# Layer 1 of a four-layer graph kernel: GpSimd's low half of x waits for the last residual of a group

## The chip, the cores and the metric

The kernel runs on one core of a Trainium2 chip, in one launch. The metric is device microseconds from the start to the end of that launch. Five engines have instruction streams of their own and meet only at semaphores: TensorE (PE in the profile), VectorE (DVE), ScalarE (ACT), GpSimd (POOL) and SyncE (SP), which here issues DMAs.

## The reference, cut to what matters

x has 64 graphs of 128 nodes with 256 features, adj has 64 matrices of 128x128. Four layers follow each other, each with a residual and a layer norm. The change lies in the second of them, which the kernel calls layer 1:

```
qk = einsum('bnd,ed->bne', x, W_qk); q, k = split(qk, 2)
v = einsum('bnd,ed->bne', x, W_v)
scores = einsum('bnd,bmd->bnm', q, k) / 8
w = softmax(sum(scores * adj, axis=-1, keepdims=True), axis=1)
x = layernorm(x + w * v)
```

The others are a hypergraph convolution (layer 0), a three-hop diffusion (layer 2) and an attention with tanh scores (layer 3).

## The kernel before

x stays in SBUF as one resident f32 tile `K.x` (`x_resident` in the profile). The work goes in groups of `GP` = 4 graphs, so there are `G` = 16 groups g = 0 to 15, and most tiles exist twice and are used in turn (p = g % 2).

f32 products are made of f16 pairs. A layer needs, for each group, a high and a low half of x, both transposed. ScalarE makes the high half (`x_high`, L1118: a copy that rounds to f16), GpSimd makes the low one (`x_low`, L1125: x minus the high half, a TENSOR_TENSOR over 128x1024 whose two inputs both lie in SBUF). SyncE then transposes each half with one DMA (`transpose_x`, L1139) into `xT_hi` and `xT_lo`, and `project` on TensorE waits for both. One product is then three matmuls (`triple`, L110 to L112). The halves are made ahead: layer 1 makes those of groups 2 to 15, and with numbers 16 and 17 those of the first two groups of layer 2.

Every engine runs a hand-written list of steps (`over_layers`): the first four unrolled, the middle ones in a hardware loop, the last ones unrolled and woven with the first steps of the next layer. The order inside a step is fixed, and an engine does not pass a wait. What belongs together in layer 1, when VectorE is in its step g:

- VectorE, step g: `weights(g-1)` copies four columns of softmax weights out of PSUM (L1282); `residual(g-1, j)` for j = 0 to 3 (L1288) computes vqk * weight + x into `l_pre`, a SCALAR_TENSOR_TENSOR of 128x256 with two inputs in SBUF; two rows of norm statistics (`norm_row`, L1039, one SBUF input); `scores(g)` (L1296, L1297 from PSUM and vqk, then L1302 reduces to `l_w`); two more rows of statistics; `maximum(g)` (L1306, L1310), `norm_variance(g-1)` (L1046 to L1053) and `softmax(g)` (L1314, L1318).
- TensorE at the same time, its step g+1: `aggregate(g)` (L1213, eight records), `project(g+1, 0)` and `project(g+1, 1)` (12 matmuls), `score_rows(g)` (L1221, waits for `l_w`), `project(g+1, 2)` and `project(g+1, 3)` (12 matmuls), `weight_columns(g)` (L1225), which releases VectorE's next L1282.
- ScalarE, step g: `x_high(g+2)`, four times `norm_apply(g-2)` (L1073), `exponentials(g)` (L1256), four times `copy_qkv(g+1)` (L1250).
- GpSimd, step g: `x_low(g+2)`, then `norm_scales(g-1)` (L1058 to L1067).
- SyncE, step g: the two transposes of group g+2, then the DMA that brings the adjacency of group g+2 (L1181).

Each `residual` adds one to the semaphore `L.pre_ok` (`l1_pre_ok`), so it stands at `upto(g, GP, 4)` = 4g + 4 when the four residuals of group g are done. `reused(g, 3)` is true in the loop and for g of 3 or more.

Of the kernel before, what the change touches and what calls it, by code (L numbers as in the profile page):

```python
# [12 lines left out]
GP = 4  # L13
# [24 lines left out]
def upto(g, per, k):  # L38

    return g * per + k  # L40
# [62 lines left out]
def reused(g, back=2):  # L103

    return not isinstance(g, int) or g >= back
# [901 lines left out]
def norm(nc, ctx, tag, deep=2, tiles=None):  # L1007

    L = Parts()
    L.deep = deep  # L1010
    tiles = tiles or ctx

    def sb(name, shape):
        made = [tiles.enter_context(nc.sbuf_tensor(f"{tag}_{name}{i}", shape, F32)) for i in range(deep)]
        return [made[p % deep] for p in range(2)]

    L.pre, L.st = sb("pre", [128, GP, D]), sb("st", [128, GP, 6])
    L.veps, L.rstd, L.nmr = (sb(name, [128, GP]) for name in ("veps", "rstd", "nmr"))
    L.mdiff, L.m2, L.dd, L.msum, L.mneg = (tiles.enter_context(nc.sbuf_tensor(f"{tag}_{name}", [128, GP], F32))
                                           for name in ("mdiff", "m2", "dd", "msum", "mneg"))  # L1020
    L.pre_ok, L.st_ok, L.agg, L.mean_ok, L.rstd_ok, L.nmr_ok, L.x_new = (
        ctx.enter_context(nc.semaphore(f"{tag}_{name}"))
        for name in ("pre_ok", "st_ok", "agg", "mean_ok", "rstd_ok", "nmr_ok", "x_new"))
    return L
# [31 lines left out]
def norm_scales(K, L, pool, g, p):  # L1056
    pool.wait_ge(L.st_ok, upto(g, GP, GP))
    pool.tensor_tensor(L.msum[:], L.st[p][:, :, 1], L.st[p][:, :, 4], ALU.add).then_inc(L.mean_ok, 1)  # L1058
    pool.wait_ge(L.mean_ok, upto(g, 2, 1))
    pool.tensor_tensor(L.mneg[:], L.msum[:], K.minus_half[:], ALU.mult).then_inc(L.mean_ok, 1)  # L1060
    pool.wait_ge(L.agg, upto(g, 4, 4))
    if reused(g, L.deep):
        pool.wait_ge(L.x_new, upto(g - L.deep, GP, GP))
    pool.tensor_tensor(L.rstd[p][:], L.veps[p][:], K.minus_half[:], ALU.pow).then_inc(L.rstd_ok, 1)  # L1064
    pool.wait_ge(L.mean_ok, upto(g, 2, 2))
    pool.wait_ge(L.rstd_ok, upto(g, 1, 1))
    pool.tensor_tensor(L.nmr[p][:], L.mneg[:], L.rstd[p][:], ALU.mult).then_inc(L.nmr_ok, 1)  # L1067
# [26 lines left out]
def front_of(shared, layer):  # L1094
    F = Parts()
    F.x_hi, F.x_lo, F.xT_in, F.xs, F.xT = shared.x_hi, shared.x_lo, shared.xT_in, shared.xs, shared.xT
    F.base = (layer - 1) * G
    F.made = 2
    F.ahead = 2 if layer < 3 else 0
    return F  # L1100


def halves_due(F, g):

    return not isinstance(g, int) or F.made <= g < G + F.ahead


def x_group(K, g):

    return K.x[:, xcols(g - G if isinstance(g, int) and g >= G else g)].rearrange("p (g d) -> p g d", g=GP)  # L1110
# [10 lines left out]
def x_low(K, F, pool, g, p):  # L1121
    pool.wait_ge(F.x_hi, upto(F.base + g, 1, 1))
    if reused(F.base + g):
        transposed(F, pool, g - 2, p)
    pool.tensor_tensor(F.xs[p][1], x_group(K, g), F.xs[p][0], ALU.subtract).then_inc(F.x_lo, 1)  # L1125


def transposed(F, eng, g, p):

    eng.wait_ge(F.xT_in[p], 16 * (F.base + g - p) + 32)  # L1130
# [12 lines left out]
def layer1(nc, K, ctx, tiles):  # L1143
# [10 lines left out]
    L = norm(nc, ctx, "l1", tiles=tiles)  # L1154
# [16 lines left out]
    F = front_of(K.F, 1)  # L1171
# [172 lines left out]
        return step, 0, 1  # L1344

    def gpsimd(pool):
        def step(g, p, has):
            q = 1 - p
            if halves_due(F, g + 2):
                x_low(K, F, pool, g + 2, p)  # L1350
            if has(-1):
                norm_scales(K, L, pool, g - 1, q)
        return step, 2, 1
# [611 lines left out]
```

## Time and profile before

| | us |
|---|---|
| three runs | 774.9, 776.5, 778.07 |
| median | 776.5 |
| the profiled execution, as timed | 778.61 |
| its span in the trace | 776.8 |
| PE busy in the span | 696.9 (90%) |
| DVE busy | 588.0 (76%) |
| ACT busy | 531.9 (68%) |
| POOL busy | 343.3 (44%) |
| mean granted TensorE clock | 0.948 |

Layer 1 fills about 303 to 446 us of the span. The first L1282 starts at 314.9 us and the sixteenth and last at 444.4 us, one for each group. TensorE's granted clock has two levels in this trace, 1.00 (2.4 GHz) and 0.50 (1.2 GHz); a number between them is a mean over a stretch.

### The profile page before, as it was taken

The page shows a single profiled execution, that of the slowest core. Times are in us where ns is not written, and L with a number is a line of the kernel's source. Part 1 is how long each engine was busy: PE and PEld are TensorE (multiplying, and loading weights), DVE is VectorE, ACT ScalarE, POOL GpSimd, SP SyncE. Part 2 cuts the span into 40 slices and gives each one's busy share as a digit, 9 for nine tenths or more (in the row PEclk, how much of TensorE's full clock was granted, in tenths as well). Part 3 has the DMA queues.
Part 4 walks back from the last instruction along what each step waited for, and adds up shares of the span by engine and source line. Part 5 has one row for each costly group of instructions (what it writes and reads, how often), then busy time and mean ns, then how long its engine had stood idle before and what let it go on. Part 6 is the DMA issues. An engine that isn't in the chain of part 4 may idle for free.

```text
span 776.8 us, 18723 instructions
## 1 busy us (share of the span) xinstructions
PE 696.9 (90%) x5654; PEld 504.1 (65%) x5654; DVE 588.0 (76%) x1744; ACT 531.9 (68%) x1177; POOL 343.3 (44%) x418
## 2 busy tenths in 40 slices
PE   5899999999999985777878589899989998999995
PEld 5677777777777753444445366566666666888874
DVE  4888888888878762777887876767676876588995
ACT  4668887767777763465555557667776776688885
POOL 2243455434344451444444425243524253677773
PEclk9999999999999997997797689999999999799998
DMA  9522032232221020643444334634343333266663
GB/s 285 154 84 70 29 109 69 73 117 83 68 68 54 2 53 30 149 83 81 95 89 100 55 55 82 83 77 87 81 82 81 81 73 65 55 164 162 162 145 128
DMA packets 168144, 71.11 MB, mean 92 GB/s; under 512 B 122260, under 2 KB 165654, under 8 KB 168088
## 3 DMA queue, kind: packets, MB, share of 16 engines
q1 hardware_dynamic: 166496, 70.41, 37.8%
q8 instruction: 28, 0.46, 0.3%
q10 hardware_dynamic: 1592, 0.01, 0.1%
q14 instruction: 28, 0.23, 0.1%
HBM read 28.46 MB, written 8.39 MB: 47 GB/s over the span
## 4 chain that ended last, share of the span: by engine, by line
PE 39%; DVE 8%; issue 6%; DMA 4%; ACT 2%; SPq 1%; DVEq 1%; POOL 0%; ACTq 0%; POOLq 0%
PE bank L110 10%; PE bank L112 10%; PE bank L111 10%; DMA xT_lo<-x_halves 4%; PE bank L1804 3%; DVE l_pre L1288 2%; DVE l_st L1039 2%; PE bank L1407 2%; PE bank L1802 1%; SPq L1139 1%; PE bank L1225 1%; PE bank L1513 1%; DVE l_w L1302 1%; DVE l_qa L1296 1%; ACT x_resident L1073 1%
## 5 line engine op out<-in xcount | busy, mean ns | idle before, releaser
L1073 ACT ACTIVATE x_resident<-l_pre,l_nmr,l_rstd 128x256 f32 (+1 forms) x256 | 136.9, 595 | 26.8 <-POOL l_nmr L1067 26.7
L1125 POOL TENSOR_TENSOR x_halves<-x_resident,x_halves 128x1024 f16<-128x1024 f16 (+1 forms) x46 | 100.1, 2176 | 39.2 <-ACT x_halves L1118 37.1
L110 PE MATMUL bank<-Wk_lo,xT_hi 128*128 128x2 f16 (+2 forms) x384 | 94.0, 274 | 4.8 <-DMA xT_lo<-x_halves 4.8
L1039 DVE BATCH_NORM_STATS2 l_st<-l_pre 128x6 f32<-128x256 f32 x256 | 96.5, 413 | 1.1
L111 PE MATMUL bank<-Wk_hi,xT_lo 128*128 128x2 f16 (+2 forms) x384 | 95.1, 273 | 0.0
L112 PE MATMUL bank<-Wk_hi,xT_hi 128*128 128x2 f16 (+2 forms) x384 | 94.7, 272 | 0.0
L983 POOL TENSOR_TENSOR hq<-hq 128x512 f32<-128x512 f32 x32 | 43.1, 1347 | 76.6 <-ACT hq L716 76.6
L1064 POOL TENSOR_TENSOR l_rstd<-l_veps,minus_half 128x4 f32<-128x4 f32 x64 | 64.6, 1009 | 24.1 <-DVE l_veps L1053 22.7
L110 PE MATMUL bank<-W2T_lo,h_hi 128*128 128x257 f16 x256 | 70.7, 276 | 2.3 <-DVE h_lo L860 1.2
L111 PE MATMUL bank<-W2T_hi,h_lo 128*128 128x257 f16 x256 | 70.8, 277 | 0.0
L112 PE MATMUL bank<-W2T_hi,h_hi 128*128 128x257 f16 x256 | 70.8, 276 | 0.0
L1729 POOL TENSOR_TENSOR l_T_lo<-l_tf,l_T_hi 128x512 f16<-128x512 f32 x16 | 18.5, 1157 | 106.6 <-ACT l_T_hi L1573 106.6
L860 DVE TENSOR_TENSOR h_lo<-hf,h_hi 128x512 f16<-128x512 f32 x64 | 44.7, 702 | 18.9 <-ACT hf L705 8.3
L1288 DVE SCALAR_TENSOR_TENSOR l_pre<-l_vqk,l_wgt,x_resident 128x256 f32<-128x256 f32 x64 | 55.0, 922 | 1.9 <-DVE l_wgt L1282 1.7
L722 ACT ACTIVATE zf<-bank 128x258 f32<-128x258 f32 x64 | 24.7, 388 | 46.2 <-PE bank L637 46.1
L705 ACT ACTIVATE hf<-bank,b_col 128x512 f32<-128x512 f32 x64 | 44.0, 687 | 16.1 <-PE bank L112 15.6
L110 PE MATMUL bank<-qkvT_lo,xT_hi 128*128 128x384 f16 x128 | 48.0, 375 | 6.2 <-PEq L527 6.2
L110 PE MATMUL bank<-xT_lo,W1T_hi 128*128 128x512 f16 x128 | 48.5, 379 | 1.6 <-DVE qkvT_lo L414 1.5
L112 PE MATMUL bank<-xT_hi,W1T_hi 128*128 128x512 f16 x128 | 48.5, 379 | 0.0
L111 PE MATMUL bank<-xT_hi,W1T_lo 128*128 128x512 f16 x128 | 48.5, 379 | 0.0
L1118 ACT ACTIVATE x_halves<-x_resident 128x1024 f16 (+1 forms) x46 | 48.4, 1052 | 0.0
L971 POOL TENSOR_TENSOR zrs<-zvar,minus_half 128x4 f32<-128x4 f32 x16 | 22.0, 1378 | 59.0 <-DVE zvar L897 59.0
(206 smaller groups left out, 2119.6 us busy)
## 6 DMA issues: line engine op xcount, KB each, us to landing
adj<-in_adj SPq DMA_DIRECT2D x32, 256.0 KB, 3.7
x_halves<-in_x SPq DMA_DIRECT2D x16, 512.0 KB, 3.7
x_resident<-in_x SPq DMA_DIRECT2D x16, 512.0 KB, 4.8
out<-x_resident SPq DMA_DIRECT2D x15, 512.0 KB, 3.2
l_adjT<-adjT_resident SPq DMA_DIRECT2D x16, 256.0 KB, 2.5
x_resident<-in_L_gnn_W SPq DMA_DIRECT2D x2, 512.0 KB, 5.7
x_resident<-in_L_gnn_Wk SPq DMA_DIRECT2D x1, 768.0 KB, 8.1
xT_hi<-x_halves SPq DMA_TRANSPOSE x48, 3.2
```

The lines of the kernel that those rows point to most:

```text
L110: nc.tensor.matmul(out, lhs[0], rhs[1], start=start, stop=False, **kw)
L111: nc.tensor.matmul(out, lhs[1], rhs[0], start=False, stop=False, **kw)
L112: return nc.tensor.matmul(out, lhs[0], rhs[0], start=False, stop=stop, **kw)
L705: act.activation(hf[:, h, :], b_hid[h % 2][:], ACT.Relu, bias=K.b1[:, h:h + 1], scale=1.0 / W_SCALE).then_inc(hf_ok, 1)
L860: dve.tensor_tensor(hs[1][:, h, :], hf[:, h, :], hs[0][:, h, :], ALU.subtract).then_inc(h_lo, 1)
L983: pool.tensor_tensor((hqs if h == HT - 1 else hq[:, 0, :])[:], hq[:, 0, :], hq[:, h, :], ALU.add).then_inc(hqs_ok, 1)
L1039: dve.bn_stats(L.st[p][:, j, :], L.pre[p][:, j, :]).then_inc(L.st_ok, 1)
L1064: pool.tensor_tensor(L.rstd[p][:], L.veps[p][:], K.minus_half[:], ALU.pow).then_inc(L.rstd_ok, 1)
L1073: act.activation(K.x[:, gcols(g, j)], L.pre[p][:, j, :], ACT.Identity, bias=L.nmr[p][:, j:j + 1], scale=L.rstd[p][:, j:j + 1]).then_inc(L. ...
L1118: act.activation(F.xs[p][0], x_group(K, g), ACT.Copy).then_inc(F.x_hi, 1)
L1125: pool.tensor_tensor(F.xs[p][1], x_group(K, g), F.xs[p][0], ALU.subtract).then_inc(F.x_lo, 1)
L1288: dve.scalar_tensor_tensor(L.pre[p][:, j, :], vqk[p][:, j, 0:D], wgt[p][:, j:j + 1], K.x[:, gcols(g, j)], ALU.mult, ALU.add).then_inc(L.pr ...
```

## The change

GpSimd's step calls a new function `low_half` in place of `x_low`. From group 3 on, it first waits until VectorE has finished the fourth residual of group g+2-3 = g-1, which is the group whose residuals VectorE makes in its own step g. The waits that `x_low` already had (ScalarE's high half, and the transposes that last read the buffer) follow. No instruction of any engine changes its place.

```
     def gpsimd(pool):
+        def low_half(g, p):
+            if reused(g, 3):
+                pool.wait_ge(L.pre_ok, upto(g - 3, GP, GP))
+            x_low(K, F, pool, g, p)
+
         def step(g, p, has):
             q = 1 - p
             if halves_due(F, g + 2):
-                x_low(K, F, pool, g + 2, p)
+                low_half(g + 2, p)
             if has(-1):
                 norm_scales(K, L, pool, g - 1, q)
```

The order of GpSimd's instructions with their waits, at the first unrolled steps of layer 1 (x_halves is the tile of the low half, next_x_hi counts ScalarE's high halves, next_xT_in0 and next_xT_in1 the landed transposes):

```order
 L1125 TENSOR_TENSOR x_halves<-x_resident,x_halves 128x1024 [waits next_xT_in0,next_x_hi]
-L1125 TENSOR_TENSOR x_halves<-x_resident,x_halves 128x1024 [waits next_xT_in1,next_x_hi]
+L1125 TENSOR_TENSOR x_halves<-x_resident,x_halves 128x1024 [waits next_xT_in1,next_x_hi,l1_pre_ok]
 L1058 TENSOR_TENSOR l_msum<-l_st 128x4 [waits l1_st_ok]
 L1060 TENSOR_TENSOR l_mneg<-l_msum,minus_half 128x4 [waits l1_mean_ok]
 L1064 TENSOR_TENSOR l_rstd<-l_veps,minus_half 128x4 [waits l1_agg]
 L1067 TENSOR_TENSOR l_nmr<-l_mneg,l_rstd 128x4 [waits l1_rstd_ok,l1_mean_ok]
-L1125 TENSOR_TENSOR x_halves<-x_resident,x_halves 128x1024 [waits next_xT_in0,next_x_hi]
+L1125 TENSOR_TENSOR x_halves<-x_resident,x_halves 128x1024 [waits next_xT_in0,next_x_hi,l1_pre_ok]
```

Group 2's low half is unchanged, those of groups 3 and later get the third wait, and the norm scales stand behind it as before. In the hardware loop of GpSimd the same wait sits on a register instruction ahead of the two old ones:

```order
 L93 ISA
+L1122 REGISTER_ALU [waits l1_pre_ok]
 L1130 ISA [waits next_x_hi]
 L1125 ISA [waits next_xT_in0]
 L1125 TENSOR_TENSOR x_halves<-x_resident,x_halves 128x1024
```

So there the new wait comes first, and the two old ones are looked at after it. Fifteen low halves get the wait: those numbered 3 to 17.

## Rows read from the trace of the kernel before

**Rows 1.** The page: granted clock in 40 slices, and the group L1288 (busy, mean ns).

```profile
PEclk9999999999999997997797689999999999799998
...
L1288 DVE SCALAR_TENSOR_TENSOR l_pre<-l_vqk,l_wgt,x_resident 128x256 f32<-128x256 f32 x64 | 55.0, 922 | 1.9 <-DVE l_wgt L1282 1.7
```

**Rows 2.** By line: duration in ns (min/median/max), first and last start in us.

```profile
L1282 DVE COPY l_wgt<-bank x16: 160/162/163, 314.9 to 444.4; 128x4 f32<-128x4 f32 x16
...
L1288 DVE SCALAR_TENSOR_TENSOR l_pre<-l_vqk,l_wgt,x_resident x64: 472/481/2399, 315.0 to 445.7; 128x256 f32<-128x256 f32 x64
```

**Rows 3.** Timeline, DVE, one unrolled step (start, length, instruction, idle before).

```profile
322.66 0.16 DVE L1282 COPY l_wgt<-bank 128x4 f32<-128x4 f32 x1 [0.63 <-PE bank L1225]
322.86 3.59 DVE L1288 SCALAR_TENSOR_TENSOR l_pre<-l_vqk,l_wgt,x_resident 128x256 f32<-128x256 f32 x4
326.37 0.74 DVE L1039 BATCH_NORM_STATS2 l_st<-l_pre 128x6 f32<-128x256 f32 x2
...
327.46 0.42 DVE L1302 TENSOR_REDUCE l_w<-l_qa 128x4 f32<-128x256 f32 x1
...
328.76 0.14 DVE L1310 TENSOR_SCALAR l_wneg<-l_wmax 4x1 f32<-4x1 f32 x1
...
330.51 0.16 DVE L1282 COPY l_wgt<-bank 128x4 f32<-128x4 f32 x1 [0.63 <-PE bank L1225]
```

**Rows 4.** Timeline, POOL, the same step.

```profile
324.04 2.13 POOL L1125 TENSOR_TENSOR x_halves<-x_resident,x_halves 128x1024 f16<-128x1024 f32 x1 [1.10 <-ACT x_halves L1118]
...
330.60 0.20 POOL L1067 TENSOR_TENSOR l_nmr<-l_mneg,l_rstd 128x4 f32<-128x4 f32 x1
```

**Rows 5.** Timeline, DVE, the last step of layer 1, without a low half beside it.

```profile
444.55 1.67 DVE L1288 SCALAR_TENSOR_TENSOR l_pre<-l_vqk,l_wgt,x_resident 128x256 f32<-128x256 f32 x4
```

**Rows 6.** Timeline, PE, the step of rows 3.

```profile
323.11 1.08 PE L1213 MATMUL bank<-l_vqk,l_adjT 128*128 128x65 f32 x8 [0.49 <-issue]
324.02 0.33 PE L110 MATMUL bank<-qkvT_lo,xT_hi 128*128 128x384 f16 x1
...
327.94 0.27 PE L1221 MATMUL bank<-ident,l_w 128*4 128x128 f32 x1 [1.80 <-DVE l_w L1302]
...
330.09 0.38 PE L1225 MATMUL bank<-ident,l_wn 4*128 4x4 f32 x2
```

**Rows 7.** Timeline, DVE, two steps in the hardware loop.

```profile
367.06 0.16 DVE L1282 COPY l_wgt<-bank 128x4 f32<-128x4 f32 x1 [1.86 <-PE bank L1225]
...
375.12 0.16 DVE L1282 COPY l_wgt<-bank 128x4 f32<-128x4 f32 x1 [0.74 <-PE bank L1225]
```

**Rows 8.** Windows: length, busy of PE, PEld, DVE, ACT, POOL; PEclk, DMA share, GB/s.

```profile
314.85:338.48 23.63, 16.70 (x105) 10.48 (x105) 21.04 (x61) 12.51 (x30) 11.21 (x15) 1.00 0.60 136
338.48:444.36 105.88, 80.95 (x400) 48.42 (x401) 83.82 (x241) 57.94 (x129) 46.14 (x60) 0.80 0.40 84
```

**Rows 9.** Timelines, POOL then DVE, step 0: low half beside scores.

```profile
310.34 2.12 POOL L1125 TENSOR_TENSOR x_halves<-x_resident,x_halves 128x1024 f16<-128x1024 f32 x1 [9.56 <-ACT x_halves L1118]
...
310.53 0.42 DVE L1296 TENSOR_TENSOR l_qa<-bank,l_vqk 128x256 f32<-128x256 f32 x1 [7.20 <-PE bank L1213]
...
310.99 0.42 DVE L1302 TENSOR_REDUCE l_w<-l_qa 128x4 f32<-128x256 f32 x1
```

**Rows 10.** Timelines, POOL then DVE, layer 3: low half beside norm statistics.

```profile
676.76 2.14 POOL L1125 TENSOR_TENSOR x_halves<-x_resident,x_halves 128x1024 f16<-128x1024 f32 x1
...
677.55 0.74 DVE L1039 BATCH_NORM_STATS2 l_st<-l_pre 128x6 f32<-128x256 f32 x2
678.33 0.59 DVE L1046 TENSOR_TENSOR l_mdiff<-l_st 128x4 f32<-128x4 f32 x1
```

**Rows 11.** Line L1139, 336 to 436 us: issue of the transposes to their landing.

```profile
DMA to landing us min/median/max: 3.0/3.1/3.9
```

**Rows 12.** Timeline, ACT, the step of rows 3.

```profile
322.92 1.04 ACT L1118 ACTIVATE x_halves<-x_resident 128x1024 f16<-128x1024 f32 x1
323.87 2.06 ACT L1073 ACTIVATE x_resident<-l_pre,l_nmr,l_rstd 128x256 f32<-128x256 f32 x4
```

## The prediction

> **What bounds the kernel now.** I read the page first, for the granted clock and the costliest groups, then the DVE, POOL and PE timelines of one step of layer 1, then the same lines where the low half of x lies beside other work. The page shows two odd things in layer 1: the clock digits fall to 6 and 7 there, and L1288 has a mean of 922 ns [rows 1], while its median is 481 ns and its maximum 2399 ns [rows 2]. So a few of its 64 instructions are very long.
>
> One step [rows 3] is a closed loop through VectorE and TensorE. The softmax weights arrive (L1282, 322.66), the four residuals take 3.59 us and end at 326.45, `l_w` follows, L1221 starts at 327.94 [rows 6], and the next L1282 at 330.51: 7.85 us in all. TensorE sat idle 1.80 us ahead of L1221, waiting for `l_w` [rows 6], so VectorE's part of the loop sets the pace. Inside it, GpSimd's low half runs from 324.04 to 326.17 [rows 4], in the middle of the residuals. In the last step, which has no low half beside it, the same four residuals take 1.67 us [rows 5]. The residuals are therefore held up while the low half runs, one of the four in each of 15 steps, and this wait is on the path that sets the end of layer 1.
>
> Which instructions of VectorE are held? With a low half at 310.34 to 312.46, L1296 (one input in PSUM) and L1302 (one input) take 0.42 us each [rows 9], as they do without it (L1302 in [rows 3]). In layer 3 two rows of statistics take 0.74 us inside a low half [rows 10], as they do alone [rows 3], but L1046, a 128x4 instruction with two SBUF inputs, takes 0.59 us and ends at 678.92, just after the low half ended at 678.90. So what is held is an instruction that reads two tensors from SBUF, until GpSimd's instruction is over.
>
> The Trainium skill says this in SBUF — State Buffer, section "Who interferes with whom": a DVE instruction with two SBUF inputs contends with a GpSimd instruction that reads SBUF, and one of them blocks fully. The rows agree.
>
> **What the change does, step by step.** Let T be the end of the four residuals of a step.
>
> 1. The hold on the residuals goes. In the unrolled steps they take 1.67 in place of 3.59 us, 1.9 us less; all 15 steps with a wait had one instruction held, so 15 x 1.9 = 28.5 us of VectorE's chain. As layer 1 runs from the first L1282 at 314.9 to the sixteenth at 444.4 [rows 2], 129.5 us for 15 periods, a mean of 8.63 us, this alone makes 101.0.
>
> 2. The low half moves to T + 0.1 (unrolled) or about T + 0.35 (loop, where a register instruction and two more waits come after the new one; an estimate: GpSimd's start behind ScalarE's high half is 0.08 us at 324.04 [rows 4, 12], and I allow the rest for the loop). It ends at T + 2.2 to T + 2.5. Beside it now lie two rows of statistics, L1296, L1302, two more rows: the kinds that [rows 9, 10] show unhurt. L1310 starts 2.31 us after T (328.76 against 326.45, [rows 3]), and L1046 just behind it. So at most 0.2 us of hold on L1046 in the loop, which delays the softmax by less: between 0 and 0.2 us x 10 = 2 us, I take 1.
>
> A sentence for a rule that speaks a little against the change: the same section of the Trainium skill says that `tensor_scalar` can enter a mode with two ports and then contends too, which would hold L1310 as well; no row here shows it beside a low half. By it the 1 us above would be up to 2 us.
>
> 3. Behind the low half on GpSimd stand the norm scales. L1067 ended 4.35 us after T before (330.80, [rows 3, 4]). The statistics they wait for end at about T + 2.1, and the low half is over at T + 2.2 to 2.5, so they slip by 0 to 0.3 us. ScalarE needs them for L1073, which starts 1.2 us after L1282 (323.87 against 322.66, [rows 3, 12]), and the next L1282 will come 1.50 + 2.57 = 4.07 us after T (next point); that is T + 5.3 against T + 4.65. Cost nothing, covered by 0.6 us.
>
> 4. The new period of VectorE's loop at full clock: L1282 to residuals 0.20, residuals 1.67, T to L1221 1.49 (326.45 to 327.94), L1221 to L1282 2.57 (327.94 to 330.51): 5.93 us. In the loop 0.15 to 0.2 more: 8.06 against 7.85 (367.06 to 375.12 [rows 7], against [rows 3]), so 6.1.
>
> 5. What is late next. **TensorE**: L1213 starts 0.45 after L1282, the projections 0.91 later, twelve matmuls take 1.96 (0.163 each: 2.15 from L1221 to L1225 holds twelve), so it is free at 3.3 us after L1282, and `l_w` is ready for it at 3.4. The idle 1.80 us shrinks to 0.1, a balance at full clock. At half clock 24 matmuls alone take 7.8 us, and a period would be TensorE's, about 10.3 us. **The low half's transpose**: the low half of group g+2 is needed by TensorE's next step. It lands at T + 2.5 + 3.1 [rows 11] = T + 5.6 in the loop. TensorE wants it 0.45 + 0.91 after the next L1282, at T + 5.4. Followed over two steps: T to project T + 5.65, project to L1282 4.5, to the next-but-one T 2.0, in all 12.1 us for two periods, 6.05 each. That is the same as VectorE's 6.1. So it costs about 0, and with the longest landing (3.9) 0.4 us in a period. **ScalarE** has at most 1.04 + 2.06 us ahead of L1256 [rows 12], from 0.3 to 3.3 us after L1282; L1256 waits for L1310, which comes 2.31 us after T, so at 4.2: it fits.
>
> 6. **The clock.** In 314.85 to 338.48 the clock was 1.00, in 338.48 to 444.36 it was 0.80 on average [rows 8]. Five periods of 7.85 (unrolled) and ten of 8.05 (loop, DVE-bound as in [rows 7]) would be 119.8 us; the trace has 129.5. The 9.7 us between are what the half clock costs. In a period of 7.85 us TensorE had some 1.8 us of waiting for `l_w` in one piece [rows 6]. With that down to about 0.1 us and TensorE busy for 90% of the period, I expect the clock to stay at 1.00 almost throughout, which gives back 9.7 us.
>
> The Trainium skill, TensorE: Matmul & The Clock Gate, section "What's actually happening", has activity release the throttle. By that the clock rises here; [rows 8] alone, with the clock down although TensorE was busy 76% of 105.88 us, would allow that it doesn't, and that is the second case below.
>
> **The sum.** 129.5 - 28.5 (hold) - 9.7 (clock) = 91.3 us for the 15 periods, the same as 5 x 5.93 + 10 x 6.1 = 90.7. With 1 us for L1046 and 0.5 for transposes that land late: 92.5. Saved 37.0. Against the profiled execution 778.61 - 37.0 = 741.6. That execution is 2.1 us above the median of the three runs, so against the median 776.5 it is 739.5. Nothing of layers 0, 2 and 3 changes; a shift of the clock's falls there is worth about 1 us either way.
>
> **The rivals.**
> - *The clock stays as it is* (40% of the time at half, mean 0.80). Then three periods of 5.93, and twelve of 1 / (0.6/6.1 + 0.4/10.3) = 7.3: 105.4 us, saved 24, 752.4. For it: the falls came although TensorE was three quarters busy [rows 8]. Against: the first stretch was 71% busy (16.70 of 23.63 us) with no fall at all, and the new period is busier than both. Chance 0.12.
> - *The low transpose becomes the bound*: landings of 3.9 us throughout, 0.4 us in each of 12 periods, 4.5 us, 744. Against: the median is 3.1 and the maximum stands alone [rows 11]. Chance 0.06.
> - *Slower: the low half holds the statistics too.* If L1039 right behind T were held until the low half ends, the chain would be 1.67 + 0.3 + 2.13 + 0.3 = 4.4 in place of 3.59 for the residual part less the statistics' overlap, say 0.45 us more in each of 15 steps, 6.8 us: 783.3. It decides as soon as L1039 beside a low half takes over 1.9 us more. The 0.74 us of [rows 10] speaks against it. Chance 0.02.
> - *The wait is never the last one* (ScalarE's high half comes later than T). The high half ends 1.3 us after L1282 [rows 12], T now comes 1.9 us after. Only then nothing changes, 776.5. Chance 0.02.
>
> **How the numbers follow.** The forecast, hold gone and clock up, has 0.78. Its own bounds: the best is the pure sum with no new cost and no slow landing, 15 x 5.93 = 89 us, saved 40.5, 736, and 1.5 for the scatter of the runs: 734.5. The upper end takes in the transposes and a part of the clock case: 752. About 0.5% (3.9 us) is what a measurement of this kernel can tell from no change. Faster 0.95, same 0.02, slower 0.03.
>
> **What the changed profile would show.** L1288 with a maximum near 490 ns and about 31 us of busy time in place of 55.0; L1125 starting 0.1 to 0.4 us after the fourth L1288; L1282 every 5.9 to 6.2 us; TensorE's idle before L1221 at 0 to 0.3 us; granted clock 1.00 from 338 on. The prediction is wrong if L1039 or L1302 grows beside the low half, if project waits for xT_lo by more than 0.3 us, or if the clock stays below 0.95.

## The result, and the profile after

| | before | after |
|---|---|---|
| median, same chip | 777.29 us (774.9 to 781.39) | 740.39 us (738.35 to 741.67) |
| ratio | | 0.9518, 95% interval 0.947 to 0.9566 |
| span of the profiled execution | 776.8 us | 736.6 us |
| layer 1, first to sixteenth L1282 | 129.51 us | 92.16 us |

The change makes the kernel 36.9 us faster by the medians; 37.0 were forecast. The page of the changed kernel, whose clock digits answer to [rows 1]:

```profile
PE 676.1 (92%) x5654; PEld 494.1 (67%) x5654; DVE 559.0 (76%) x1744; ACT 531.1 (72%) x1177; POOL 341.2 (46%) x418
...
PEclk9999999999999998799999799999999999999998
```

The digits of 6 and 7 in the middle are nearly gone. By line, over layer 1 (duration in ns min/median/max, first and last start in us), the answer to [rows 2]:

```profile
L1282 DVE COPY l_wgt<-bank x16: 160/163/163, 315.4 to 407.5; 128x4 f32<-128x4 f32 x16
...
L1288 DVE SCALAR_TENSOR_TENSOR l_pre<-l_vqk,l_wgt,x_resident x64: 475/479/486, 315.6 to 408.9; 128x256 f32<-128x256 f32 x64
...
L1310 DVE TENSOR_SCALAR l_wneg<-l_wmax x16: 141/142/143, 313.4 to 405.7; 4x1 f32<-4x1 f32 x16
```

The longest of the 64 residuals takes 486 ns, where before it took 2399. One unrolled step on VectorE (start, length, instruction, idle before it), the same one as in [rows 3]:

```profile
321.33 0.16 DVE L1282 COPY l_wgt<-bank 128x4 f32<-128x4 f32 x1 [0.63 <-PE bank L1225]
321.53 1.67 DVE L1288 SCALAR_TENSOR_TENSOR l_pre<-l_vqk,l_wgt,x_resident 128x256 f32<-128x256 f32 x4
323.12 0.74 DVE L1039 BATCH_NORM_STATS2 l_st<-l_pre 128x6 f32<-128x256 f32 x2
...
324.22 0.42 DVE L1302 TENSOR_REDUCE l_w<-l_qa 128x4 f32<-128x256 f32 x1
...
325.51 0.14 DVE L1310 TENSOR_SCALAR l_wneg<-l_wmax 4x1 f32<-4x1 f32 x1
325.58 0.14 DVE L1046 TENSOR_TENSOR l_mdiff<-l_st 128x4 f32<-128x4 f32 x1
...
327.26 0.16 DVE L1282 COPY l_wgt<-bank 128x4 f32<-128x4 f32 x1 [0.64 <-PE bank L1225]
```

GpSimd and TensorE in that step, answering to [rows 4] and [rows 6]:

```profile
323.28 2.13 POOL L1125 TENSOR_TENSOR x_halves<-x_resident,x_halves 128x1024 f16<-128x1024 f32 x1 [1.66 <-DVE l_pre L1288]
...
327.35 0.20 POOL L1067 TENSOR_TENSOR l_nmr<-l_mneg,l_rstd 128x4 f32<-128x4 f32 x1
```

```profile
321.79 1.08 PE L1213 MATMUL bank<-l_vqk,l_adjT 128*128 128x65 f32 x8 [0.49 <-issue]
...
324.69 0.27 PE L1221 MATMUL bank<-ident,l_w 128*4 128x128 f32 x1
```

The residuals end at 323.20 and the low half begins 0.08 us later. It runs beside L1039, L1296 (0.41 us, not shown) and L1302, and none of them grew. L1221 has no idle time ahead of it, where it had 1.80 us. The step takes 5.93 us (321.33 to 327.26), to the hundredth what was worked out.

Where the 37.35 us of layer 1 went is read from windows of both kernels. After the stretch and its length come busy us and count of PE, PEld, DVE, ACT and POOL, then the granted clock, the DMA share and GB/s. First the kernel before from its first L1282 to its sixteenth, then the kernel after, likewise:

```profile
314.85:444.36 129.51, 97.65 (x505) 58.90 (x506) 104.86 (x301) 70.45 (x158) 57.35 (x74) 0.84 0.44 94
```

```profile
315.39:407.55 92.16, 80.27 (x505) 51.40 (x506) 76.74 (x301) 69.60 (x158) 55.55 (x74) 0.99 0.63 131
```

The same 301 VectorE instructions took 28.1 us less: the hold (28.5 forecast). By difference, the rest of the 37.35, 9.2 us, is what the clock no longer costs (9.7 forecast); it rose from 0.84 to 0.99, and the same 505 matmuls are 17.4 us shorter, about half of it on the path.

The profiled spans differ by 40.2 us, 3.3 more than the medians. Behind the sixteenth L1282 the kernel before has 332.4 us left and the one after 329.1; in the nine profiled executions of this document whose kernels are all alike from there on (e5 to e8 aside) it was 328.8 to 332.5, and e1, which has the new wait too, has 332.2. The last 120 us had a clock of 0.93 in the profile of before and 0.97 in that of after. So I take those 3.3 us for scatter in layers 2 and 3 and not for the change; one profile of each kernel doesn't settle it.

### The profile page after: what moved, and what is told of

The parts are those of the page before. It is cut to its first block, busy times and chain, and to the rows that moved or that the text cites. A ratio compares the mean times of both kernels' runs of the same rounds, so it can differ in the third digit from the quotient of the medians.

```text
span 736.6 us, 18723 instructions
## 1 busy us (share of the span) xinstructions
PE 676.1 (92%) x5654; PEld 494.1 (67%) x5654; DVE 559.0 (76%) x1744; ACT 531.1 (72%) x1177; POOL 341.2 (46%) x418
## 4 chain that ended last, share of the span: by engine, by line
PE 42%; DMA 6%; DVE 3%; issue 2%; POOL 2%; ACT 1%; SPq 1%; DVEq 0%; POOLq 0%; ACTq 0%
PE bank L110 11%; PE bank L112 11%; PE bank L111 11%; DMA xT_lo<-x_halves 6%; PE bank L1809 3%; PE bank L1412 2%; POOL x_halves L1125 2%; PE bank L1807 1%; DVE l_pre L1288 1%; SPq L1139 1%; PE bank L1518 1%; DVE l_st L1039 1%; ACT l_mid_hi L1572 1%; PE bank L1213 1%; PE bank L1225 0%
## 5 line engine op out<-in xcount | busy, mean ns | idle before, releaser
L1039 DVE BATCH_NORM_STATS2 l_st<-l_pre 128x6 f32<-128x256 f32 x256 | 96.5, 414 | 1.1
L110 PE MATMUL bank<-qkvT_lo,xT_hi 128*128 128x384 f16 x128 | 42.6, 333 | 7.8 <-PEq L527 6.2
L110 PEld LDWEIGHTS bank<-Wk_lo,xT_hi 128*128 128x128 f16 x384 | 35.0, 97 | 19.7 <-DMA xT_lo<-x_halves 3.8
```

What stands on the lines that cost most here:

```text
L110: nc.tensor.matmul(out, lhs[0], rhs[1], start=start, stop=False, **kw)
L1039: dve.bn_stats(L.st[p][:, j, :], L.pre[p][:, j, :]).then_inc(L.st_ok, 1)
```

## The experiments

The theory: a VectorE instruction with two inputs in SBUF and GpSimd's low half cannot run together; whichever starts second is held until the other is over. (So the two engines meet there too, and not only at semaphores, as the opening has it.) The change takes the low half away from the residuals, and TensorE, which no longer waits, keeps its clock. Rivals: it is the wait itself, or the moment at which the transposes start, that helps (transfers or queues, not the hold); the clock's fall has a cause of its own; the loop has slack in which the low half could go elsewhere. A time is the median of four executions (ten for e7), and a ratio is to the kernel before, timed beside that run. "Period" is from one L1282 to the next.

**e1, wait for the second residual.** Against the changed kernel:

```diff
-                pool.wait_ge(L.pre_ok, upto(g - 3, GP, GP))
+                pool.wait_ge(L.pre_ok, upto(g - 3, GP, 2))
```

> The changed kernel, but the low half waits for the second residual of the same group in place of the fourth. Theory of the hold (an instruction with two SBUF inputs and GpSimd's low half exclude each other, whoever has begun goes on): the low half starts while the third residual runs, as in the kernel before, and the fourth is held by about 1.9 us in each of 15 steps; L1288 has a maximum near 2.4 us, 774 to 779 us. Rival (any ordering by pre_ok helps, because the transposes of the low half come later and collide less): most of the gain stays, 740 to 755 us.

Measured: 744.43 us, ratio 0.9569 (0.9527 to 0.9612). So nearly all of the gain stayed, and the expectation of a hold in every step was wrong. Timeline of e1, DVE and then POOL, in the first period and in a later one:

```profile
314.06 3.55 DVE L1288 SCALAR_TENSOR_TENSOR l_pre<-l_vqk,l_wgt,x_resident 128x256 f32<-128x256 f32 x4
...
321.87 1.68 DVE L1288 SCALAR_TENSOR_TENSOR l_pre<-l_vqk,l_wgt,x_resident 128x256 f32<-128x256 f32 x4
```

```profile
315.13 2.20 POOL L1125 TENSOR_TENSOR x_halves<-x_resident,x_halves 128x1024 f16<-128x1024 f32 x1 [3.65 <-DVE l_pre L1288]
...
323.10 2.43 POOL L1125 TENSOR_TENSOR x_halves<-x_resident,x_halves 128x1024 f16<-128x1024 f32 x1 [1.14 <-DVE l_pre L1288]
```

Only the first period has the hold (a residual of 2353 ns, period 7.81 us). In the later one the low half starts at 323.10 and is itself 0.30 us longer: it was GpSimd that was held. The residuals start 0.40 us apart, so the fourth began at 321.87 + 1.19 = 323.06, 0.04 us ahead. In the kernel before, the low half of [rows 4] started 1.38 us after L1282, and the fourth residual 1.39 after it. So whoever starts first keeps going, and a shift of 0.05 us moved 1.9 us from VectorE's path to GpSimd's slack. The median low half of e1 is 2429 ns in layer 1.

The 0.05 us do not come from the second residual, though the row names L1288. That residual was over at 322.75, and ScalarE's high half, the other wait of this low half, ended later, at 322.97 (timeline of e1, ACT):

```profile
321.93 1.04 ACT L1118 ACTIVATE x_halves<-x_resident 128x1024 f16<-128x1024 f32 x1
```

In the kernel before, the low half started 0.08 us behind the high half, in e1 0.13 us. So what e1 changed in this step is one more wait to look at, and that sufficed.

In the kernel before, the held residual is the fourth in 13 of the 15 steps and the third in two. In seven steps its low half is longer too, 2203 to 2438 ns: it began while one residual was running, was held for that one's rest, and then went ahead of the next. In e1's later steps there is no next residual. The rest of e1's loss to the changed kernel is one period of 8.62 us, in which a transpose came late (0.92 us) and the clock fell.

**e2, wait for the third residual** (`upto(g - 3, GP, 3)`).

> As before, with the third residual. Theory of the hold: the fourth residual has begun when GpSimd is released (0.1 us in unrolled steps, 0.35 us in the loop, after the third ends), so the low half is what waits; no L1288 above 0.5 us. The low half starts at the end of the fourth residual at the earliest, up to 0.3 us sooner than with the fourth, and the loop's period falls from 6.17 to 6.1 us: 738 to 741 us. Rival (GpSimd wins whoever began): the fourth is held again, 770 to 778 us.

Measured: 739.74 us, ratio 0.9533 (0.95 to 0.9566), layer 1 91.82 us, longest residual 486 ns. In an unrolled step the low half starts at 322.82 and the fourth residual at 322.66 (two residuals from 322.26, 0.40 apart), so GpSimd is again the second and is held (2.31 us), with 0.16 us to spare. In the loop it starts 1.92 to 1.97 us after L1282, 0.4 us behind the fourth, and takes its usual 2.13 us. The time is that of the changed kernel.

**e3, the low half beside the norm's variance.** The wait is for `l_w` of the step instead, so that the low half starts later:

```diff
-                pool.wait_ge(L.pre_ok, upto(g - 3, GP, GP))
+                pool.wait_ge(w_ok, upto(g - 2, 1, 1))
```

> The low half waits for l_w of the same step (L1302, w_ok) in place of the fourth residual, 1.5 us later. Theory of the hold: it then lies beside L1046, which has two SBUF inputs of 128x4, from 2.4 us after the residuals; L1046 grows from 0.14 to about 1.5 us and holds the softmax behind it, and the transpose lands 1.5 us later: a period of 7.4 to 7.8 us, 760 to 768 us, more if the clock falls too. Rival (only large instructions are held): the transpose alone, 6.7 us a period, 747 to 750 us.

Measured: 759.63 us, ratio 0.977 (0.9722 to 0.9817); layer 1 takes 113.67 us at a clock of 0.91. Timeline of e3 in one step, DVE, then POOL:

```profile
349.93 0.14 DVE L1310 TENSOR_SCALAR l_wneg<-l_wmax 4x1 f32<-4x1 f32 x1
350.00 1.52 DVE L1046 TENSOR_TENSOR l_mdiff<-l_st 128x4 f32<-128x4 f32 x1
...
352.91 0.16 DVE L1282 COPY l_wgt<-bank 128x4 f32<-128x4 f32 x1 [0.58 <-PE bank L1225]
```

```profile
349.38 2.12 POOL L1125 TENSOR_TENSOR x_halves<-x_resident,x_halves 128x1024 f16<-128x1024 f16 x1 [3.76 <-DVE l_w L1302]
```

L1046 has 4 elements per partition and took 1.52 us, until the low half was over (351.50). Its median over layer 1 is 1283 ns, against 143 ns after the change. So it is the two SBUF inputs that matter and not the size. Nineteen of the 37 us are lost again by a wait that ends some 1.4 us later (the low half starts 1.77 us behind the residuals, not 0.36). They are no measure of the hold: the 15 L1046 took 13.1 us more in all, while layer 1 grew by 21.5, and TensorE now waits for transposes that land late as well (8.1 us in nine waits of PE for `xT_lo`, against 1.1 after the change). e11 below holds nothing, has its transposes about as late, and loses 13.2 us in layer 1. No run parts the two shares. L1310, one row ahead, ran beside the low half at 0.14 us; the rule of the Trainium skill weighed in the prediction, that a `tensor_scalar` can contend too (SBUF — State Buffer, "Who interferes with whom"), is bound there to conditions on the operands, and this 4x1 instruction was not held.

**e4, hardly any low half.** The kernel before, whose low half in layer 1 covers 2 of 256 columns at its old place:

```diff
-                x_low(K, F, pool, g + 2, p)
+                x_low(K, F, pool, g + 2, p, 2)
```

> The kernel before, without the new wait, but in layer 1 GpSimd makes only 2 of the 256 columns of each low half (the rest of the low halves made there is stale, so the low parts of x are left out of the products). The place of everything else stays. Theory of the hold: without a long GpSimd instruction beside the residuals they take 1.7 to 1.9 us, TensorE waits less, the clock goes up: L1282 every 5.9 to 6.1 us, 736 to 741 us. Rival (the gain is from the new place of the low half's transposes): here they come earlier still, so 770 to 777 us.

Measured: 739.39 us, ratio 0.9526 (0.9485 to 0.9567); layer 1 is 91.41 us at a clock of 1.00, longest residual 486 ns. GpSimd has no new wait here and its transposes start earlier, not later, and still the whole gain is there. That excludes the rival that the wait or a later start of the transposes helps by itself. It also bounds what the change leaves in layer 1: 92.16 against 91.41, 0.75 us.

**e5, e6, e8, e7: VectorE's chain made longer without a hold.** Against the changed kernel, with reduces of `l_pre` into a spare tile right behind the residuals of all 16 groups (so L1288 is L1289 in them, and so on); e5 has one of 128x1024, e6 two, e8 one of 128x1024 and one of 128x256, e7 this:

```diff
+            dve.tensor_reduce(spare[p][:, 0, :], L.pre[p][:], AX.X, ALU.add)
+            dve.tensor_reduce(spare[p][:, 1, 0:2], L.pre[p][:, 0:2, :], AX.X, ALU.add)
```

> The changed kernel with one extra instruction of VectorE behind the fourth residual in each of the 16 groups: a TENSOR_REDUCE over l_pre, 128x1024, one SBUF input, result unused, about 1.1 us. It puts back about half of what the hold had cost in VectorE's chain, with nothing held. 16 x 1.1 = 17.6 us: 758 us if the clock stays at 1.00 in layer 1. Theory (the clock falls when TensorE's wait for l_w grows to about 2 us): still 1.00, TensorE waits 1.1 us, 755 to 760 us. Rival (any wait beyond 0.5 us brings it down): 763 to 768 us, clock near 0.85 in layer 1.

> As e5 with two such instructions, about 2.1 us, a little over the 1.9 us that the hold cost, with nothing held. At a clock of 1.00 this is 740 + 16 x 2.1 = 774 us. Theory (the 9.7 us of half clock came from TensorE's waiting and not from what GpSimd did): TensorE waits about 2.1 us again, the clock falls to about 0.8 in layer 1 as before, and the time is 779 to 786 us. Rival (the half clock had to do with the hold itself, or with chance): clock 0.95 to 1.00, 772 to 776 us.

> As e7 with 128x1024 and 128x256, together about 1.55 us. It lies between e5 (wait of TensorE 1.3 us, clock 0.99 in layer 1) and e7. If the clock goes by the length of TensorE's wait, it shows on which side 1.6 us falls: 764 to 767 us and clock 0.97 or more where it holds, 770 to 776 us and below 0.9 where it falls.

> The changed kernel with a spare instruction of VectorE over 128x1024 (1.22 us in e5) and one over 128x512 (an estimate: 0.6 to 0.7) behind the fourth residual, unused results. Together they lengthen VectorE's chain by 1.85 to 1.95 us, which is what the hold of the kernel before cost (3.59 against 1.67), but nothing is held and each step of layer 1 is otherwise that of the changed kernel. Theory (hold and clock are two effects, and the clock follows from TensorE's wait for l_w of 1.8 us or more): L1282 every 8.0 us at full clock, 8.5 to 8.8 on average, clock in layer 1 near 0.8, 774 to 782 us, the time of the kernel before. Rival (the clock fell for another reason that the hold brings): 15 x 1.9 = 28.5 us over the changed kernel, 767 to 770 us, clock near 1.00.

| | first period longer by | us, ratio (95%) | layer 1, clock | TensorE's wait for `l_w`, steps at full clock, last step aside |
|---|---|---|---|---|
| after | 0 | 740.39 | 92.16, 0.99 | 0 to 0.2 |
| e5 | 1.25 | 760.88, 0.9786 (0.9733 to 0.9838) | 110.16, 0.99 | 1.1 to 1.4 |
| e8 | 1.57 | 767.65, 0.9858 (0.9789 to 0.9926) | 115.30, 0.98 | 1.46 to 1.73 |
| e7 | 1.84 | 779.64, 1.0025 (0.9992 to 1.0058) | 125.67, 0.86 | 1.73 to 2.23 |
| e6 | 2.37 | 797.88, 1.027 (1.0225 to 1.0315) | 144.02, 0.83 | 2.3 to 2.8 |

Windows of the layer in e8 and in e7 (columns as above), then one step of e7 on VectorE:

```profile
315.69:430.99 115.30, 80.18 (x505) 50.65 (x506) 99.76 (x331) 69.44 (x158) 56.14 (x74) 0.98 0.48 105
```

```profile
313.92:439.59 125.67, 94.35 (x505) 57.79 (x506) 103.77 (x331) 70.29 (x158) 56.12 (x74) 0.86 0.44 97
```

```profile
347.35 1.67 DVE L1289 SCALAR_TENSOR_TENSOR l_pre<-l_vqk,l_wgt,x_resident 128x256 f32<-128x256 f32 x4 [0.16 <-DVE l_wgt L1283]
349.05 1.22 DVE L1294 TENSOR_REDUCE l_spare<-l_pre 128x4 f32<-128x1024 f32 x1
350.19 0.67 DVE L1295 TENSOR_REDUCE l_spare<-l_pre 128x2 f32<-128x512 f32 x1
```

In e7 the residuals stay at 1.67 us; nothing is held. Yet a chain that is nearly as much longer as the hold was (first unrolled period 7.78 us, 7.81 in the kernel before) gives about the time of the kernel before, and the clock falls with it. By the medians e7 takes 39.3 us more than the changed kernel, and the added work accounts for 16 x 1.84 = 29.4. In its one trace layer 1 is 125.67 us long against 129.51; of the 33.5 us over the changed kernel 15 x 1.84 = 27.6 are the chain, so 5.9 the clock, where the kernel before lost 9.2. So a long chain of VectorE by itself brings the clock down, with nothing held, and the change got the clock back by shortening that chain; that the chain explains all 9 us in layer 1 isn't shown, about two thirds are. From e8 to e7 VectorE's busy time grows by 4.0 us and the layer by 10.4. e6 came out slower than expected for two reasons that its rows give: a reduce of 128x1024 takes 1.22 us and not the 1.05 I had set, and the clock's part was larger (57.5 us over the changed kernel, of which 16 x 2.37 = 37.9 are the chain).

**e9, the wait only in the hardware loop; e10, only in the unrolled steps.** (`g` is a plain integer in the unrolled steps alone.) Against the changed kernel:

```diff
-            if reused(g, 3):
+            if not isinstance(g, int):
```

```diff
-            if reused(g, 3):
+            if isinstance(g, int) and g >= 3:
```

> The new wait only in GpSimd's hardware loop, 10 of the 15 steps. Theory of the hold: the five unrolled steps keep a residual of 2.4 us and take 7.85 us each, the ten in the loop 6.17; at full clock 15 periods take 101 us in place of 92.2, 749 us; up to 753 if the clock falls near the unrolled steps. Rival (the wait matters at the start, where DMA is busiest): little of the gain is here, over 765 us.

> The new wait only in the unrolled steps of GpSimd (low halves 3 and those after the loop, 5 of 15). Theory: ten periods keep the hold, at 8.05 us at full clock or 9.1 with the half clock as in the kernel before, five take 5.94; 766 us, down to 760 if the clock falls less. With e9 the two gains should come to within 3 us of the gain of the whole change.

Measured: e9 749.17 us, ratio 0.9648 (0.9619 to 0.9676), layer 1 101.17 us; e10 765.61 us, ratio 0.9849 (0.9824 to 0.9874), layer 1 119.67 us. Saved in layer 1 against before: 28.3 and 9.8 us, 38.2 together, where both at once save 37.35; by the medians beside their own runs of before (776.06), 26.9 and 10.5. The parts add up; neither enables the other. TensorE's waits for `l_w` (its timeline), first in e9's unrolled steps, then in e10's loop:

```profile
319.09 0.27 PE L1221 MATMUL bank<-ident,l_w 128*4 128x128 f32 x1 [1.88 <-DVE l_w L1302]
326.94 0.27 PE L1221 MATMUL bank<-ident,l_w 128*4 128x128 f32 x1 [1.80 <-DVE l_w L1302]
334.79 0.27 PE L1221 MATMUL bank<-ident,l_w 128*4 128x128 f32 x1 [1.82 <-DVE l_w L1302]
```

```profile
353.18 0.27 PE L1221 MATMUL bank<-ident,l_w 128*4 128x128 f32 x1 [2.02 <-DVE l_w L1302]
362.88 0.27 PE L1221 MATMUL bank<-ident,l_w 128*4 128x128 f32 x1 [2.09 <-DVE l_w L1302]
372.43 0.27 PE L1221 MATMUL bank<-ident,l_w 128*4 128x128 f32 x1 [2.32 <-DVE l_w L1302]
```

The unrolled steps of e9 (7.85 us apart) keep the full clock; the three rows of e10's loop are 9.70 and 9.55 apart. The loop steps of e10 in which the clock did not fall take 8.04 to 8.06 us.

**e11, is there slack for a later low half?** e4's small low half, but behind the last instruction of the norm's variance:

```diff
+                if reused(g + 2, 3):
+                    pool.wait_ge(L.agg, upto(g - 1, 4, 4))
-                x_low(K, F, pool, g + 2, p)
+                x_low(K, F, pool, g + 2, p, 2)
```

> As e4 (GpSimd makes only 2 of the 256 columns of each low half in layer 1, so nothing is held), but that small instruction waits for l_veps of the same step (L1053), about 3.0 us after the residuals; it and the transpose behind it then come 0.9 us later than in the changed kernel and 3 us later than in e4. It tests what is next late. Theory (the transpose has about no slack over two steps): project waits for xT_lo, a period of 6.4 to 6.6 us in place of 6.17, 742 to 748 us. Rival (the transpose has slack, VectorE's chain alone sets the pace): 738 to 741 us, no wait for xT_lo.

Measured: 753.04 us, ratio 0.9701 (0.9665 to 0.9736), layer 1 105.39 us at 0.96, periods near 7.0 us. That is worse than either theory had it. Timeline of e11, in order of time, TensorE, GpSimd, the queue of SyncE and TensorE again:

```profile
347.20 0.27 PE L1222 MATMUL bank<-ident,l_w 128*4 128x128 f32 x1
...
348.76 0.26 POOL L1125 TENSOR_TENSOR x_halves<-x_resident,x_halves 128x8 f16<-128x8 f16 x1 [4.75 <-DVE l_veps L1053]
...
349.04 1.23 SPq L1140 DMA_TRANSPOSE xT_lo<-x_halves  x1
...
352.24 0.33 PE L110 MATMUL bank<-qkvT_lo,xT_hi 128*128 128x384 f16 x1 [1.05 <-DMA xT_lo<-x_halves]
...
354.20 0.27 PE L1222 MATMUL bank<-ident,l_w 128*4 128x128 f32 x1
```

L1053 stands on VectorE behind the reduce that waits for TensorE's L1222. So the low half now follows this step's L1222 by 1.56 us, its transpose lands in time for the next step's projections 3.5 us later, and L1222 follows 1.96 us behind those: 7.0 us around, in one step. I had counted a loop of two steps, with one more period (6 us) of room; since an engine does not pass a wait, the new one closed a loop of one step. There is no slack behind the place that e3 tried.

## Why the prediction was right, step by step

**Step 1, the hold (28.5 us): right.** The residuals take 1.67 us in every step and VectorE's busy time fell by 28.1 us. That it is a hold between the two engines is shown from three sides: by e4 (shrink GpSimd's instruction where it stands, and the gain is there), by e3 (move it, and another instruction of the same kind grows), and by e1 (shift by 0.05 us, and the other engine pays).

**Step 2, the low half's new place: right in the place, too dear in its cost.** It starts 0.08 us behind the residuals in the unrolled steps. In the loop it starts 0.36 us behind them (0.35 forecast); timelines of DVE and POOL there:

```profile
347.24 0.87 DVE L1288 SCALAR_TENSOR_TENSOR l_pre<-l_vqk,l_wgt,x_resident 128x256 f32<-128x256 f32 x2
```

```profile
348.47 2.13 POOL L1125 TENSOR_TENSOR x_halves<-x_resident,x_halves 128x1024 f16<-128x1024 f16 x1 [2.15 <-DVE l_pre L1288]
```

And L1046 in that step, again on DVE:

```profile
350.49 0.14 DVE L1046 TENSOR_TENSOR l_mdiff<-l_st 128x4 f32<-128x4 f32 x1
```

L1046 was to pay 1 us in all; its longest of 15 is 145 ns. It begins 0.11 us before the low half ends (350.60) and ends 0.03 us behind it, much as the held L1046 of e3 did (351.52 against 351.50). So there is no cost, and hardly any room either.

**Step 3, the norm scales: right.** L1067 ends at 327.55, 0.29 us after L1282; the bound allowed 1.2 us before ScalarE wants it, and ScalarE fits.

**Steps 4 and 5, the period: 5.93 exact in the unrolled steps, 6.1 a little short in the loop.** There the periods are 6.16 to 6.24 in most steps. The 6.1 was rounded down from rows that carry 6.17: the hold in the loop was 1.88 us (3.55 against 1.67), off a period of 8.05. That 8.05 was read from a step of [rows 7] whose clock was not 1.00 but 0.74, with TensorE waiting only 0.33 us for `l_w`; it held by luck, as e10's loop steps at full clock take 8.04 to 8.06. I put 0.5 us on transposes that land late; the waits of the changed kernel in layer 1 (us in total, times, longest) give 1.1:

```profile
POOL x_halves L1125 <- DVE l_pre L1288: 32.0, 15, 4.3
...
DVE l_wgt L1282 <- PE bank L1225: 11.7, 16, 0.9
...
PE bank L110 <- DMA xT_lo<-x_halves: 1.1, 4, 0.6
```

Most of that falls in one period of 6.63 us at the loop's start, with a landing of 4.4 us. That the two-step loop through `xT_lo` is about as tight as VectorE's own was right: it is on the chain that ended last now (the chain of the changed kernel, start, length, what):

```profile
347.64 0.48 DVE l_pre L1288
...
348.47 2.14 POOL x_halves L1125
350.63 3.12 DMA xT_lo<-x_halves
...
353.87 0.33 PE bank L110
```

But it isn't what sets 6.17: e4, whose low half takes 0.2 us, has the same loop period of 6.17. There TensorE still waits 0.12 to 0.15 us for `l_w` in the loop, so in e4 VectorE's chain sets the pace; in the changed kernel most of these steps have no such wait, so the two engines are about level. No run took that apart. The prediction's two sums, 91.3 and 90.7, were called the same, and with its 1.5 us give 92.8 and 92.2; the 92.5 lies between. 1 us too much for L1046 and about 0.7 too little for the loop's periods and the transposes cancel by luck: 92.16 measured.

**Step 6, the clock (9.7 us): right in size, with a finer condition than was argued.** The windows give 0.99 and 9.2 us; the clock still falls in the last step (its period has 0.87), as in every run. The second case, clock unchanged (752.4 us), didn't come. The prediction argued from 1.8 us of waiting per step, but by [rows 8] the unrolled steps with just that wait kept the full clock. What separates them is finer: over before, e7, e8, e9 and e10, the last step aside, no wait for `l_w` of up to 1.95 us was followed by a fall. Of the 21 waits of 1.96 us and more, 18 were, within 1.2 us; three in e10's loop were not (2.00 and twice 2.32 us). Windows of the kernel before, up to its first wait of over 2 us (2.04, ended at 343.87) and behind it:

```profile
341.00:343.80 2.80, 0.83 (x6) 0.29 (x3) 2.80 (x7) 0.63 (x2) 1.09 (x1) 1.00 0.65 123
343.80:346.50 2.70, 2.63 (x9) 1.35 (x10) 1.83 (x11) 1.41 (x5) 1.36 (x3) 0.52 0.60 157
```

0.52 is all but the lower of the two levels, 1.2 GHz. That wait isn't the only way to a fall: e1 has one, e11 two and e3 five in steps without any wait for `l_w`, most of them just behind a wait for `xT_lo` (0.92 us in e1, 0.79 in e11). So what decides, the single wait, the idle time of the whole step or the period, these runs don't separate.

**The rivals.** Transposes as the bound (744): 1.1 us of waits, not 4.5. Statistics held (783.3): L1039 stayed at 0.74 us for two. The wait never last (776.5): it ended GpSimd's idle time 15 times out of 15, 32.0 us in all.

No version was clearly better than the change: e2 (739.74 us) is the same within its interval, and so is e4, which leaves out nearly all of the low half. So all but 0.75 us of what the low half cost layer 1 is gone. In layer 3 the hold is still there after the change: twelve L1046 take 0.42 to 1.72 us, each until 0.02 to 0.03 us after the low half beside it ends, 9.5 us more in all; no run shows what of that is on the path.

## What to carry to other kernels

When the longest instruction of a line is several times its median, look at what GpSimd runs at that moment: in this kernel two engines that each read two SBUF tensors held one another, and the price was the rest of the instruction that had started first, however small the other. Put the long one beside work that has one SBUF input or reads PSUM, and order the two by a wait, not by luck: here 0.05 us of start time, the price of one more wait, decided 1.9 us per step. Before moving it, follow the loop through its consumer with every in-order wait on the way; and where TensorE waits for such a chain for about 2 us in each step, as here, a shorter chain can pay twice, the second time by the clock.

## What the runs showed of the hardware that I had not expected

- The hold works both ways, and the first to start keeps going: 2.43 us for a low half that started 0.04 us after a residual, and 2.35 us for a residual that started second.
- It does not scale with the held instruction: a 128x4 TENSOR_TENSOR went from 0.14 to 1.52 us.
- A low half that had to wait for the rest of one residual still went ahead of the next: 2.44 us for the low half and 2.35 us for the residual in the same step of the kernel before.
- The clock's fall is steep in the length of the chain: 1.57 us more per step cost 23.1 us in layer 1 at a clock of 0.98, and 1.84 us more cost 33.5 us at 0.86.
